# A decoder block over 64 sequences: the layer norm's last step as subtract and multiply, without the scaled and negated mean

## The reference

```python
def _layernorm(x, axis=-1, eps=1e-05):
    m = jnp.mean(x, axis=axis, keepdims=True)
    v = jnp.var(x, axis=axis, keepdims=True)
    return (x - m) / jnp.sqrt(v + eps)
...
x = x + attn(_layernorm(x))            # 16 heads of 16, causal, a slope times the distance as bias
x = x + xattn(_layernorm(x), ctx)      # 16 heads over 120 context tokens
x = x + tanh(_layernorm(x) @ W @ W1 @ W2 + bias)
```

## Time and profile before

| | |
|---|---|
| median of 3 runs | 2377.55 us (2377.23 to 2383.47) |
| the profiled execution | 2373.22 us |
| its span, first to last instruction | 2371.5 us |
| TensorE busy | 2229.0 us, 94% |
| VectorE, ScalarE, GpSimd busy | 1708.8, 1416.2, 719.2 us |
| mean granted TensorE clock | 0.984 |

### The profile page before, as it was taken

How to read it: one execution, slowest core, us unless ns; L and a number is a source line. 1 busy time by engine, 2 the same in 40 slices (tenths; PEclk the granted TensorE clock), 3 DMA queues, 4 the chain that set the end, 5 groups by cost and what they waited for, 6 DMA issues and landing times.

```text
span 2371.5 us, 67224 instructions
## 1 busy us (share of the span) xinstructions
PE 2229.0 (94%) x22072; PEld 1848.5 (78%) x22072; DVE 1708.8 (72%) x3710; ACT 1416.2 (60%) x3066; POOL 719.2 (30%) x1372
## 2 busy tenths in 40 slices
PE   4799999999999999999999999999999999999985
PEld 3588887887887887887888888788788788788764
DVE  4477777777777777777877877777777777777762
ACT  2466666666666666666666666666666666666651
POOL 3132333333233233233233233323323323323321
PEclk9899999999999999999999999999999999999995
DMA  6533433433443443443343344344344344344320
GB/s 134 124 95 106 109 107 95 118 106 98 115 107 89 109 120 85 113 111 96 103 116 98 104 107 108 95 116 107 98 113 110 86 109 120 88 111 111 98 73 23
DMA packets 167370, 244.83 MB, mean 103 GB/s; under 512 B 22176, under 2 KB 90512, under 8 KB 164248
## 3 DMA queue, kind: packets, MB, share of 16 engines
q1 hardware_dynamic: 165660, 244.22, 39.0%
q10 hardware_dynamic: 1664, 0.01, 0.1%
HBM read 53.13 MB, written 33.56 MB: 37 GB/s over the span
## 4 chain that ended last, share of the span: by engine, by line
PE 75%; DVE 8%; issue 5%; POOL 4%; DMA 3%; ACT 2%; SPq 2%; DVEq 0%; POOLq 0%; ACTq 0%
PE ps_misc L555 14%; PE ps_misc L541 14%; PE ps_score L630 7%; PE ps_max L612 5%; PE ps_score L639 5%; PE ps_score L629 4%; PE ps_attend L654 4%; PE ps_misc L684 4%; DVE neg_max_s L975 4%; PE ps_max L600 3%; PE ps_misc L525 3%; PE ps_misc L699 3%; PE ps_attend L673 2%; DMA q_stack<-neg_max_t_s 2%; PE ps_misc L566 2%
## 5 line engine op out<-in xcount | busy, mean ns | idle before, releaser
L813 ACT ACTIVATE probs<-ps_score 128x384 f32<-128x384 f32 x1024 | 476.2, 495 | 145.7 <-PE ps_score L630 142.7
L975 DVE TENSOR_REDUCE neg_max_s<-ps_max 128x2 f32<-128x512 f32 (+1 forms) x768 | 479.2, 679 | 5.7 <-PE ps_max L594 4.5
L820 ACT ACTIVATE xprobs<-ps_score 120x512 f32<-120x512 f32 x512 | 292.5, 597 | 251.6 <-PE ps_score L639 213.5
L1113 POOL TENSOR_SCALAR ve_LN<-mv_LN 128x2 f32<-128x2 f32 x192 | 37.0, 193 | 1112.7 <-DVE mv_LN L997 1092.7
L983 DVE TENSOR_REDUCE neg_max_x<-ps_max 128x4 f32<-128x480 f32 x512 | 316.6, 650 | 21.3 <-PE ps_max L612 9.6
L630 PE MATMUL ps_score<-q_stack,k_stack 128*128 128x256 f32 x1024 | 321.6, 335 | 0.0
L629 PE MATMUL ps_score<-q_stack,k_stack 128*128 128x128 f32 x1024 | 292.6, 286 | 17.7 <-DMA q_stack<-neg_max_t_s 12.3
L629 PEld LDWEIGHTS ps_score<-q_stack,k_stack 128*128 128x128 f32 x1024 | 194.7, 190 | 62.9 <-DMA q_stack<-neg_max_t_s 29.3
L1141 POOL TENSOR_TENSOR res<-res,chain_n 128x512 f32<-128x512 f32 x64 | 81.6, 1275 | 410.2 <-ACT chain_n L858 410.2
L639 PE MATMUL ps_score<-xq_stack,xk_stack 128*120 128x256 f32 x1024 | 201.6, 309 | 4.4 <-DMA xq_stack<-neg_max_t_x 3.5
L600 PE MATMUL ps_max<-k_stack,q_stack 127*128 127x256 bf16 x1024 | 194.8, 281 | 4.5 <-DVE neg_max_s L975 0.7
(11 more groups left out here) (147 smaller groups left out, 5379.2 us busy)
## 6 DMA issues: line engine op xcount, KB each, us to landing
k_stack<-k_nat SPq DMA_DIRECT2D x192, 256.0 KB, 3.8
q_stack<-q_nat SPq DMA_DIRECT2D x192, 256.0 KB, 3.7
xq_stack<-q_nat SPq DMA_DIRECT2D x192, 256.0 KB, 3.7
xk_stack<-scr_xk SPq DMA_DIRECT2D x192, 128.0 KB, 2.7
x_in<-in_x SPq DMA_DIRECT2D x64, 256.0 KB, 2.7
scr_xk<-k_nat SPq DMA_DIRECT2D x32, 512.0 KB, 3.0
out_y<-res SPq DMA_DIRECT2D x64, 256.0 KB, 2.2
ctx_in<-in_ctx SPq DMA_DIRECT2D x32, 240.0 KB, 3.0
```

Of the source, the lines that this page charges most:

```text
L813: act.activation(probs[:, h % 8, :], bank_of("SCORE", i, b, h)[:, P:4 * P], ACT.Exp)\
L820: act.activation(xprobs[0:C, at:at + 2, :], blocks(bank_of("XSCORE", i, b, u))[0:C], ACT.Exp).then_inc(sem("xprobs_ready"), 1)
L975: dve.tensor_reduce(o, ins, AX.X, ALU.max, negate=True).then_inc(sem("max_taken"), 1)
```

## The change

`mr` and `nmr` are no longer made. The last operation of each half subtracts the mean (column 0 of `mv`) and multiplies by `rstd`, instead of multiplying by `rstd` and adding `nmr`. The semaphore of the small operations counts two per layer norm instead of four.

```diff
         ln_sb = {n: (sb(f"st_{n}", [P, NB, 6]), sb(f"mv_{n}", [P, NB, 2]), sb(f"ve_{n}", [P, NB]),
-                     sb(f"rstd_{n}", [P, NB]), sb(f"mr_{n}", [P, NB]), sb(f"nmr_{n}", [P, NB]))
+                     sb(f"rstd_{n}", [P, NB]))
...
-                    wait(pool, s, 4, i, b, 1)
+                    wait(pool, s, 2, i, b, 1)
                     pool.tensor_tensor(rstd[:, :], ve[:, :], half[:, :], ALU.pow).then_inc(sem(s), 1)
-                    wait(pool, s, 4, i, b, 2)
-                    pool.tensor_tensor(mr[:, :].unsqueeze(2), mv[:, :, 0:1], rstd[:, :].unsqueeze(2), ALU.mult)\
-                        .then_inc(sem(s), 1)
-                    wait(pool, s, 4, i, b, 3)
-                    alone(pool)
-                    pool.tensor_scalar(nmr[:, :], mr[:, :], -1.0, 0.0, ALU.mult, ALU.add).then_inc(sem(s), 1)
-                    wait(pool, s, 4, i, b, 4)
+                    wait(pool, s, 2, i, b, 2)
                     free(i, b)
                     alone(pool)
                     for a in range(NB):
-                        last = pool.tensor_scalar(dst[:, a, :], src[b % 2][:, a, :], rstd[:, a:a + 1],
-                                                  nmr[:, a:a + 1], ALU.mult, ALU.add)
+                        last = pool.tensor_scalar(dst[:, a, :], src[b % 2][:, a, :], mv[:, a, 0:1],
+                                                  rstd[:, a:a + 1], ALU.subtract, ALU.mult)
```

More of the change, by code:

```diff
@@ L1105, in normalise @@
             def normalise(kind, src, dst, free, bias_name, biased):
-                st, mv, ve, rstd, mr, nmr = ln_sb[kind]
+                st, mv, ve, rstd = ln_sb[kind]
                 def f(i, b, _):
```

## The result

The changed kernel takes 2472.98 us (2470.59 to 2473.7, 4 runs) against 2377.57 (2377.23 to 2383.47, 4 runs): 1.0395 times as long, 95% interval 1.0379 to 1.041. It is 95 us slower where 3 us less were forecast, outside the range of 2369 to 2380 us, and also beyond the 2401 us that the slower rival had for its dearest operation.

What follows compares the result with a forecast made beforehand. The transfer of the maxima, ending after LN2, was taken to bound loop steps, which gain 0; 0.3 + 0.05 + 0.3 + 0.15 + 2.0 = 2.8 us outside them takes 2377.55 to 2374.7 us, range 2369 to 2380.

Steps and rivals of the forecast that it cites:

- the slower rival: New last step on GpSimd dearer than 560 ns, costing time past 0.39 us extra; two passes give 2401 us; chance 0.08.
- the two paths: In each loop step LN2 and the transfer of the maxima run side by side; the transfer ends last, steady steps gain nothing.
- The rival that the idle matmul engine's waits are the gain: TensorE's stall for LN2 gained in full, 0.67 us in 62 steps, 41 us, 2336 us; full or large gain chance 0.07.
- The cost of the new last step: Subtract/multiply on 128x256 on GpSimd taken as 560 ns, like multiply/add; far end 1120 ns as two passes.
- The dearer operation: Rival that the new last step on GpSimd costs more than 560 ns, past its threshold of 0.39 us extra; chance 0.08.
- LN1 and LN3 "late already": In the loop TensorE takes both results late already, so LN1 1.34 us and LN3 0.67 us sooner gain nothing.

Runs made afterwards that it cites:

- e1: Changed kernel with multiply and add as the last step's pair, so not a layer norm: 2374.62 us, 0.998 of the kernel before.
- e9: Kernel before with one transfer of the self-attention maxima instead of two, layer norms untouched: 2368.85 us, 0.9961.
- e10: Kernel before with the single transfer of the maxima and the mean negated ahead of the power, last step add then multiply: 2348.84 us, 0.9881.
- m1: Kernel before with 48 GpSimd instructions after its last one, trying operation pairs: on 128x256 mult/add took 555 ns, subtract/mult 1228.
- e7: Kernel before with one more small operation, a copy of the negated product, in LN2's chain alone: 2394.48 us, 1.0076.
- e5: Kernel before with the change in LN2 alone: 2417.86 us, 1.017.
- e4: Kernel before with the change in LN1 alone: 2398.01 us, 1.0084.
- e6: Kernel before with the change in LN3 alone: 2396.97 us, 1.0086.
- m2: Kernel before with further GpSimd forms after its last instruction, on 128x256: single subtract, add or mult 926 ns, tensor_tensor 723 to 724.
- e2: Kernel before with the mean negated ahead of the power and the last step adding it, then multiplying by the reciprocal: 2372.81 us, 0.9978.
- e3: Kernel before without the negation, the last step multiplying by the reciprocal, then subtracting mean times reciprocal: 2528.95 us, 1.0634.

## Why the prediction was wrong, point by point

**What bounds the kernel: right.** The reading of the two paths, LN2's stall in front and the transfer's 0.4 us behind it, gave e1's time within its range, its unchanged turn and its moved wait, and e9 with e10 shows it from the other side. The rival that the idle matmul engine's waits are the gain, with 2336 us, fell with e1: 44 of 50.6 us of waits were removed and 3 us came back. The sentence of the Trainium skill that it leaned on (Perfetto Trace Analysis, Optimization Strategies) asks to "optimize those engines that are blocking the critical path"; the prediction left these last words out, and by e1 GpSimd was not alone in blocking it.

**The cost of the new last step: the step that failed.** "So 560" was taken from the row of another pair of operations. The two small operations went and the gap became 0.21 us, as said; but the step costs 1222 ns in all 384 instances, 0.66 us more, above even the far end that I had bounded it with (1120, two passes). m1 shows that the pair alone does this, and e1 shows it on the kernel's own operands: mult/add takes 555 ns there. I had argued that subtract stands nearer to multiply and add than to a power; in these rows nearness in arithmetic says nothing, add/add is as slow as subtract/mult. In m1 two pairs of two operations differ fourfold, 0.8 and 3.3 ns an element. The Trainium skill has one rate for loop bodies of two or fewer operations, 1.03 cycles an element (GPSIMD Engine Reference, section 3.1, Elementwise — side-by-side cycle accounting). The prediction named section 7, whose note gives such bodies no price and sets those with a compare apart, so "whatever they are" was more than it says. For this instruction the measurement decides against one rate.

**The chances.** The dearer operation had 0.08, on the ground that nothing in the rows but the power spoke for it. There was nothing against it either: no row had that pair.

**The slower rival: right in kind, too small.** Its threshold stood well (e7: slack 0.15 instead of 0.1), and for LN2 alone its formula gives 2 x 0.66 - 0.77 = 0.55 us a step, where e5 measured 0.54. But it charged LN2 only. **LN1 and LN3 "late already"** is the second step that failed. That TensorE did not wait for them said nothing of how much room there was: it took LN1's result 0.08 us after it was there and LN3's 0.25 to 0.47 us after, little beside a chain 0.65 us longer, and e4 and e6 show 0.33 and 0.30 us a step. For chains that get shorter this did no harm, as e1 shows. With 0.19 more for all three together, 0.15 of it for LN1 behind LN2, the step is 1.36 us longer.

**The sum of what happened.** 56 loop steps of 1.36 us are 76 us, and some 10 are the clock, below. That leaves 9 of the 95 us for the other eight steps and the layer norms at the two ends, which at the loop's rate would make 11 or somewhat more. These were not measured one by one; the start alone differs from run to run (the first `MAX_T` is loaded at 54.1 us in the profile before and at 60.2 in m2's, whose instructions there are the same), so the sum closes only to some microseconds.

## What to carry to other kernels

An operation that no row of the trace shows has no price: do not lend it that of another pair of the same instruction, but run it alone first; a ladder of forms behind the kernel's last instruction is one run. On GpSimd, write a tensor_scalar with two operations as mult/add, add/mult or mult/mult, which took 555 ns on 128x256 where the other pairs took 1220 to 1228 (negate the small operand first, as e2 does, instead of subtracting in the large instruction). And where two paths end within some tenths of each other, shortening either alone gives next to nothing (5 and 8 us here, 28 for both); find the second before judging the first, and shorten both. A path that is not waited for is not thereby safe to lengthen: read how long its result lies ready before it is taken.

## What the runs showed of the hardware that I had not expected

**A single operation is slower than two.** 926 ns for one multiplication, addition or subtraction on 128x256 by a per-partition scalar, 555 to 558 for mult/add with two.

**A per-partition scalar costs time of its own.** On 128x256 add/mult takes 554 ns with two of them and 482 with one and a constant; mult/add takes 404 with two constants. That is some 75 ns for each.

**Longer stalls cost clock.** In the loop of the kernel before, the granted clock of TensorE is at its full level (2.4 GHz) throughout. In the changed kernel it fell to the lower one (0.50, 1.2 GHz) for short stretches, ten of them between 240 and 2270 us. Windows of the changed kernel (busy of each engine, then PEclk): one such stretch, and four steps from load to load of `MAX_T`:

```profile
505.80:509.20 3.40, 3.37 (x16) 3.37 (x17) 1.25 (x4) 1.19 (x3) 3.08 (x4) 0.50 0.43 111
...
465.20:501.11 35.91, 33.30 (x339) 27.55 (x337) 25.82 (x56) 21.45 (x47) 13.81 (x15) 1.00 0.35 92
501.11:539.31 38.20, 36.21 (x353) 30.80 (x352) 27.28 (x59) 22.62 (x49) 13.81 (x15) 0.96 0.40 107
539.31:575.21 35.90, 33.29 (x339) 27.54 (x338) 25.80 (x56) 21.45 (x47) 13.81 (x15) 1.00 0.35 92
575.21:612.37 37.16, 34.73 (x353) 29.29 (x352) 27.29 (x59) 22.63 (x49) 13.81 (x15) 1.00 0.41 110
```

The second and the fourth step do the same work; the one with the fall takes 38.20 - 37.16 = 1.04 us more. Ahead of the fall at 505.8 TensorE had stood 1.36 us before `LN2_T` and 0.52 us before `XHEADS_OUT` part 1, where it had stood 0.69 us and not at all in the kernel before; all ten falls begin at this place, 4.5 to 4.9 us behind the load of `MAX_T`. Ten such steps are the 10 us of the sum.

By the profiles, one of each kernel, the falls come with LN2's stall. Past 300 us there are 14 in e3 (a stall of 1.6 us before `LN2_T`), 9 in the changed kernel, 5 in LN1 with LN2 and 5 in LN2 alone (1.3 us each), and none in e7 (1.0 us), LN1 alone, LN3 alone, e1 and e2 (0.7 us or less). But the three kernels with 1.3 us do not have the same count, and between 200 and 300 us one fall stands also in e1 and in e7, and two in LN1 alone. So the length of this one stall does not settle it by itself; what else counts stays open.
